# A four-layer graph network on one core: k's weight split on VectorE, x loaded later, output biases as two fp32r rows, and layer 2 that makes messages first

## The reference

```
x = LN(x + layer0(x))   # 8-head attention, bias from edge weights; two inner layer norms
x = LN(x + layer1(x))   # GCN: relu(segment_sum((x W)[src] * norm) + b)
x = LN(x + layer2(x))   # relational: h_all = x @ rel_W[r] + rel_b[r]; msg = h_all[src, type]
                        # agg = segment_sum(msg, dst) / max(deg, 1); LN(x + x self_W + self_b + agg);
                        # then gelu MLP 512-1024-512 and LN
x = LN(x + layer3(x))   # edge attention, 8 heads; MLP 512-256-512
```

## Time and profile before

| what | value |
|---|---|
| median of 3 runs | 628.55 us (623.87 to 629.28) |
| profiled execution, own time | 631.25 us |
| its span, first to last instruction | 629.5 us |
| mean granted TensorE clock | 0.959 |
| PE busy | 563.1 us (89%) |
| DVE busy | 384.2 us (61%) |
| ACT busy | 242.9 us (39%) |
| POOL busy | 238.4 us (38%) |

### The profile page before, as it was taken

One profiled execution on the slowest core, in us unless ns is written; L12 is line 12 of the kernel. 1 busy time (PEld: TensorE's weight loads), 2 busy tenths in 40 slices (PEclk: granted clock), 3 DMA queues, 4 the chain that ended last, 5 costly groups with the idle time before them and its releaser, 6 DMA issues.

```text
span 629.5 us, 7530 instructions
## 1 busy us (share of the span) xinstructions
PE 563.1 (89%) x2433; PEld 355.0 (56%) x2448; DVE 384.2 (61%) x939; ACT 242.9 (39%) x510; POOL 238.4 (38%) x210
## 2 busy tenths in 40 slices
PE   6998999993988999987999899996999998999691
PEld 2443444462843446666767688864877784445560
DVE  7986988993069868967646413134245416884736
ACT  3100700062247864573642221213433116885434
POOL 6565666668554004307213152333152664000000
PEclk8999999997999999997999899997999998999986
DMA  8720000022556000247222142244251844000001
GB/s 275 315 71 2 0 0 0 0 69 79 186 154 180 4 2 0 68 106 179 75 76 86 48 133 68 67 134 125 77 183 52 247 128 126 0 1 2 1 1 67
DMA packets 29383, 53.32 MB, mean 85 GB/s; under 512 B 4945, under 2 KB 6429, under 8 KB 28838
## 3 DMA queue, kind: packets, MB, share of 16 engines
q1 hardware_dynamic: 15436, 26.09, 14.0%
q0 software_dynamic: 11968, 19.96, 11.0%
q10 hardware_dynamic: 1946, 6.85, 3.3%
HBM read 50.73 MB, written 2.17 MB: 84 GB/s over the span
## 4 chain that ended last, share of the span: by engine, by line
PE 67%; DVE 17%; ACT 6%; issue 5%; POOL 2%; DMA 2%; ACTq 0%; DVEq 0%; POOLq 0%
PE bank L478 18%; PE bank L455 11%; PE bank L456 11%; PE bank L457 11%; PE bank L568 4%; PE bank L545 3%; PE bank L552 3%; DVE h L1040 2%; DVE sp L1193 2%; PE bank L447 2%; POOL edge_bias L364 1%; ACT waste L762 1%; ACT gap L762 1%; DVE h L1049 1%; DVE h L1048 1%
## 5 line engine op out<-in xcount | busy, mean ns | idle before, releaser
L341 POOL TENSOR_TENSOR wl<-wraw,wh 128x512 fp32r<-128x512 f32 (+1 forms) x82 | 106.9, 1324 | 98.7 <-DMA wh<-w 33.1
L478 PE MATMUL bank<-hot 128*128 128x512 bf16 x529 | 118.9, 383 | 5.6 <-DVE hot L1097 4.8
L478 PEld LDWEIGHTS bank<-hot 128*128 128x128 bf16 x544 | 53.4, 99 | 70.8 <-DVE hot L1097 6.2
L364 POOL DMA_INDIRECT edge_bias<-ewn,cell_at x68 | 76.5, 1125 | 44.3 <-DVE cell_at L1091 19.1
L455 PE MATMUL bank<-th,wl 128*128 128x512 f32 x104 | 43.4, 417 | 15.0 <-POOL wl L341 12.4
L455 PE MATMUL bank<-wh,tl 128*128 128x512 f32 x112 | 46.2, 412 | 3.0 <-DVE tl L1008 3.0
L457 PE MATMUL bank<-wh,th 128*128 128x512 f32 x112 | 44.4, 397 | 0.0
L456 PE MATMUL bank<-wl,th 128*128 128x512 f32 x112 | 44.4, 397 | 0.0
L456 PE MATMUL bank<-tl,wh 128*128 128x512 f32 x104 | 42.8, 411 | 0.0
L457 PE MATMUL bank<-th,wh 128*128 128x512 f32 x104 | 42.3, 407 | 0.0
L777 ACT ACTIVATE sp<-sp,peak 128x512 f32<-128x512 f32 x44 | 31.7, 720 | 25.7 <-DVE peak L1193 25.4
(11 more groups left out here) (194 smaller groups left out, 1083.2 us busy)
## 6 DMA issues: line engine op xcount, KB each, us to landing
wraw<-w SPq DMA_DIRECT2D x26, 256.0 KB, 2.9
wh<-w POOLq DMA_DIRECT2D x6, 1024.0 KB, 5.8
keyb<-edge_keys ACTq DMA_DIRECT2D x4, 1088.0 KB, 12.0
wh<-w_rel POOLq DMA_DIRECT2D x4, 1024.0 KB, 5.8
wraw<-w_rel SPq DMA_DIRECT2D x16, 256.0 KB, 2.7
wraw<-w_qkv SPq DMA_DIRECT2D x12, 256.0 KB, 6.4
wraw<-w_o SPq DMA_DIRECT2D x8, 256.0 KB, 3.0
wh<-w_o POOLq DMA_DIRECT2D x2, 1024.0 KB, 5.8
```

What stands on the lines that cost most here:

```text
L341: pool.tensor_tensor(wl[n % WSLOTS][:, k, 0:width], wraw[:, q % 3, 0:width], wh[n % WSLOTS][:, k, 0:width], ALU.subtract).then_inc(s["w_lo ...
L364: pool.indirect_dma_start(out=bias_dram, out_offset=bass.IndirectOffsetOnAxis(ap=cell_at[:, c:c + 1], axis=0), in_=ewn[:, c:c + 1], in_off ...
L478: mm = pe.matmul(ps(name)[:], hot[:, slot, 0, i * P:(i + 1) * P], hot[:, slot, 1 + kind, :], start=False, stop=last, skip_group_check=True)
```

## The change

1. **k's weight.** It leaves the list of raw quarters. Once POOL has taken the low part of x^T from `y`, SP loads all of w0_k into `y`; ACT rounds it early. DVE takes its low part after marking duplicates and ahead of unpacking. POOL's `low(1)` is gone.
2. **x's load** waits for `bias_loaded` too; ahead of it stands one more raw quarter.
3. **Output biases.** Each row is loaded twice, into two neighbouring partitions of `rows` (cleared by POOL). DVE makes `add2`: high part in the even, low part in the odd partition (`second` is -1 on odd partitions, so row = -high + raw). One fp32r matmul of 2 partitions takes the place of the fp32 matmul of 1. For layer 3's b3_2 the same is done on 2 partitions, and ACT issues its load later.
4. **Layer 2.** message(r, i) = x tile i times W_r (12 matmuls); DVE adds the relation's bias row to it in PSUM; ACT and DVE split it; gather(r, k) adds C_r's source tile k times the message tile to all four agg2 banks (12 matmuls). The degrees and L680 are gone, and so are DVE's two memsets and the split rows of x. The bias rows are broadcast to all partitions (4 x 256 KB), behind z1. `counth` of relation 0 is split after the layer norm, not ahead of z1's eviction; the mask's three parts are spread over rounds 1 to 3.

```diff
@@ SP
-            for q in range(3, 7):
+            raw(3)
+            eng.wait_ge(s["x_low"], K)
+            eng.dma_start(y[:], weights["w0_k"].rearrange("(k p) n -> p k n", p=P)).then_inc(s["ld_k"], 16)
+            for q in range(4, 7):
                 raw(q)
...
+            eng.wait_ge(s["rows_clear"], 1)
             for n, name in enumerate(("b0_o", "b0_1", "b2_self", "b2_2")):
-                eng.dma_start(par[32 * n:32 * n + 1, 4, :], rows_of[name]).then_inc(ld_par[4], 16)
+                eng.dma_start(rows[32 * n:32 * n + 2, :], rows_of[name].to_broadcast([2, D])).then_inc(s["ld_bias"], 16)
+            raw(7)
             eng.wait_ge(s["dups_done"], 1)
+            eng.wait_ge(s["bias_loaded"], 16)
             eng.dma_start(x[:], x0.rearrange("(i p) d -> p i d", p=P)).then_inc(s["ld_x"], 16)
...
-                    eng.wait_ge(s["deg_zero"], 1)
+                    wait_full(eng, ("z1", K - 1))
                     for r in range(4):
-                        eng.dma_start(rel_rows[32 * r:32 * r + 1, :], rel_b[r:r + 1, :]).then_inc(s["ld_rel"], 16)
+                        eng.dma_start(rel_add[:, r, :], rel_b[r:r + 1, :].to_broadcast([P, D])).then_inc(s["ld_rel"], 16)
@@ POOL
-            low(1)
@@ PE
-                row = slice(32 * n, 32 * n + 1)
-                pe.matmul(ps(name)[:], ones[row, :].bitcast(F32), par[row, 4, :], start=True, stop=False)
+                row = slice(32 * n, 32 * n + 2)
+                pe.matmul(ps(name)[:], ones[row, :], add2[row, :], start=True, stop=False)
...
+            def gather(r, k, tiles, last=False):
+
+                pe.wait_ge(s["msgl_ready"], T * r + k + 1)
+                pe.wait_ge(s["countl_ready"], T * r + k + 1)
+                for i in tiles:
...
+                    pe.matmul(ps(name)[:], countl[:, k, cut], msgh[:, r % 2, k, :], start=r == 0 and k == 0, stop=False)
+                    pe.matmul(ps(name)[:], counth[:, k, cut], msgl[:, r % 2, k, :], start=False, stop=False)
+                    mm = pe.matmul(ps(name)[:], counth[:, k, cut], msgh[:, r % 2, k, :], start=False, stop=last)
+                return mm
...
+            for i in range(T):
+                row_tile("self2", i, 6, 2, turned(1, i))
+                if i == 0:
+                    w_ready(7)
+                message(0, i)
+                if i < 2:
+                    turn(1, x, 3, i + 2)
+            for r in range(3):
+                w_ready(8 + r)
                 for k in range(T):
...
+                    message(r + 1, k)
+                    gather(r, k, range(T)).then_inc(s["msg_used"], 1)
+            for i in range(T):
+                for k in range(T):
+                    mm = gather(3, k, [i], k == T - 1)
+                finish(mm, ("agg2", i))
@@ ACT
+            def count_high(r, i):
+
                 if r:
...
+                    act.wait_ge(s["msg_used"], T * (r - 1) + i + 1)
+                act.copy(counth[:, i, :], counts[:, r // 2, r % 2, i, :]).then_inc(s["counth_ready"], 1)
@@ DVE
+            dve.wait_ge(s["ld_bias"], 64)
+            bias_rows(rows[:], slice(0, P), 0)
+            for f in range(K):
+                dve.wait_ge(s["k_high"], f + 1)
+                dve.tensor_tensor(wl[1][:, f, :], y[:, f, :], wh[1][:, f, :], ALU.subtract).then_inc(s["k_low"], 1)
...
-            count_low(0)
...
             for r in range(1, 4):
...
+                for i in range(T):
+                    message_add(r, i)
+                    if r == 1:
+                        mask_of(i)
+                    if r == 3:
+                        mask_and_log(i)
+                    message_low(r, i)
+                    count_low(r, i)
```

More of the change, by code:

```diff
@@ L97, in psum_plan @@
     tiles("turn1", 0)
-    n = 0
     for r in range(4):
-        for f in range(5):
-            use(("z2", r, f), 4 + n % 4)
-            n += 1
+        for i in range(4):
+            use(("msg", r, i), 4 + i)
     tiles("self2", 0)
@@ L131 @@
 W_LAST = {"w0_q": ("q0", 3), "w0_k": ("k0", 3), "w0_v": ("v0", 3), "w0_o": ("o0", 3), "w0_1": ("f0", 3), "w1": ("g1", 3),
-          "w2_self": ("self2", 3), "w2_rel3": ("agg2", 3), "w2_1a": ("hid2", 3), "w2_1b": ("hid2", 7), "w2_2a": ("f2", 3), "w2_2b": ("f2", 3),
+          "w2_self": ("self2", 3), **{f"w2_rel{r}": ("msg", r, 3) for r in range(4)}, "w2_1a": ("hid2", 3), "w2_1b": ("hid2", 7), "w2_2a": ("f2", 3), "w2_2b": ("f2", 3),
           "w3_q": ("q3", 3), "w3_k": ("k3", 3), "w3_v": ("v3", 3), "w3_o": ("o3", 3), "w3_1": ("hid3", 1), "w3_2": ("f3", 3)}
@@ L625, in _ @@
                     turn(1, x, 3, i - 2)
-            def source_ready(k):
-                if k >= 2:
-                    turn(1, x, 3, k)
-                pe.wait_ge(s["rowl_ready"], T + k + 1)
-                pe.wait_ge(s["countl_ready"], k + 1)
-            def degrees(r):
-                begin(("z2", r, 4))
-                for k in range(T):
-                    pe.matmul(ps(("z2", r, 4))[:], ones[:], countl[:, k, :], start=k == 0, stop=False)
-                    mm = pe.matmul(ps(("z2", r, 4))[:], ones[:], counth[:, k, :], start=False, stop=k == T - 1)
-                finish(mm, ("z2", r, 4))
@@ L809, in weight_high @@
                 act.copy(wh[n][:, k, :], wraw[:, q % 3, :]).then_inc(s["w_high"], 1)
-            for q in range(7):
+            for q in range(4):
+                weight_high(q)
+            act.wait_ge(s["ld_k"], 16)
+            for f in range(K):
+                act.copy(wh[1][:, f, :], y[:, f, :]).then_inc(s["k_high"], 1)
+            for q in range(4, 7):
                 weight_high(q)
@@ L1116, in _ @@
             dve.sem_inc(s["const_ready"], 1)
-            link(dve.memset(ones[:].bitcast(F32), 1.0))
+            link(dve.tensor_scalar(ones[:], iota[:, 0:P], 0.0, 1.0, ALU.mult, ALU.add))
             link(dve.memset(keyb[:, E:], -1.0))
@@ L1162, in _, with bias_rows @@
             dve.sem_inc(s["dups_done"], 1)
+            def bias_rows(raw, rows_, count):
+                dve.tensor_copy(add2[rows_, :], raw).then_inc(s["add2_ready"], 1)
+                dve.wait_ge(s["add2_ready"], count + 1)
+                dve.scalar_tensor_tensor(out=add2[rows_, :], in0=add2[rows_, :].bitcast(F32), scalar=second[rows_, :], in1=raw, op0=ALU.mult,
+                                         op1=ALU.add).then_inc(s["add2_ready"], 1)
+            dve.wait_ge(s["ld_ident"], 16)
+            link(dve.tensor_reduce(second[:], ident[:, 1::32], AX_X, ALU.add))
+            link(dve.tensor_scalar(second[:], second[:], -1.0, None, ALU.mult))
+            dve.wait_ge(s["ld_bias"], 64)
+            bias_rows(rows[:], slice(0, P), 0)
+            for f in range(K):
+                dve.wait_ge(s["k_high"], f + 1)
+                dve.tensor_tensor(wl[1][:, f, :], y[:, f, :], wh[1][:, f, :], ALU.subtract).then_inc(s["k_low"], 1)
             for b in range(8):
```

225 lines of the change are left out of this document (95 added, 130 removed).

## The result

| | before | after |
|---|---|---|
| median | 627.86 us (4 runs, 623.87 to 629.28) | 605.93 us (4 runs, 604.03 to 607.49) |
| profiled execution, own time | 631.25 us | 605.63 us |
| its span, first to last instruction | 629.5 us | 603.9 us |
| mean granted TensorE clock | 0.959 | 0.963 |

The ratio is 0.9667, with a 95% interval of 0.9618 to 0.9716. The forecast of 599.0 was 6.9 us too low; its range, 590 to 609, holds the time. The profiled executions differ by 25.6 us where the terms made 29.5. The medians differ by 21.9, because the profiled execution before lay 3.4 us above its median and the one after did not.

What follows compares the result with a forecast made beforehand. PE's matmuls were taken as the price in most stretches, its idle time as the rest. Terms 7.4 + 2.3 + 3.1 + 13.4 + 3.3 = 29.5 off the median 628.55 gave 599.0 us, range 590 to 609.

Steps and rivals of the forecast that it cites:

- k's split, 7.4: Ahead of attention: k no longer waits for POOL's scatters and subtractions, so scores start at 171.1, 7.4 us gained (4 to 10).
- the forecast's fear of it: Product v: its weight is ready between 155 and 161 while PE asks at 160, so PE might wait for it.
- o0 and the end of layer 1, 2.3 + 3.1: 2.3 us from o0's bias rows and DVE's memsets; 3.1 (1 to 4) from g1 following z1 directly.
- The 0.7 charged for collisions: End of layer 1: g1's tiles meet POOL's w2_self and rel0 subtractions on DVE's two-input adds, 0.7 us taken off.
- PE's work in layer 2, 18.4: Layer 2, PE alone: degrees, three rounds, mask round, idle time, L680 and self2's bias cost go, 18.4 us gained.
- its cover: Layer 2's added DVE and ACT work is hidden, each result used a round later, unless a step takes DVE over 5.44 us.
- The charge of 5 for DVE beside POOL: End of layer 2 and its norm: two POOL stretches block DVE's two-input operations, costing 5 us (0 to 9).
- The forecast's sign of a DVE operation of over 3 us in that norm: In the norm after layer 2, a DVE operation beside POOL would take over 3 us.
- w2_2b's lateness, charged at nothing: Behind layer 2: w2_2b's turn comes 2 us late, but not if the norm was late already; no cost charged.
- The biases, 3.3 each in self2 and f2: Four bias rows each in self2 and f2, 0.82 us saved per row, 3.3 us gained in each.
- late weights and the shared port take more: Rival: both POOL blocks at 9, attention's DVE operations hit, v's weight late; 16 to 22 us gained, 610; chance 0.18.

Runs made afterwards that it cites:

- counts_ahead: Changed kernel with relation 0's counts split ahead of z1's evictions again, not behind the layer norm; 609.65 us against 632.8 for the kernel before, ratio 0.9612.
- best2: Changed kernel with banks 0 to 3 unpacked first, POOL's cpl subtractions ahead of w2_self's transfer, and adds x + b behind layer 2's norm; 591.27 us, ratio 0.9409.
- dve_loaded: Changed kernel with three added DVE subtractions in each of 12 steps of layer 2; 608.19 us against 632.8 for the kernel before, ratio 0.9572.
- adds_later: Changed kernel with POOL's four adds x + b put behind the transfer of w2_1b instead of ahead of w2_1a's; 598.85 us, ratio 0.952.
- undo_k: Changed kernel with k's weight as raw quarters split by POOL again and x loaded early again (parts 1 and 2 undone); 610.88 us, ratio 0.9708.
- q_first: Changed kernel with DVE unpacking banks 0 to 3 ahead of the bias rows and k's low part; 602.93 us, ratio 0.9618.
- bias_fp32: Changed kernel with the bias matmuls plain fp32 on one partition again (part 3 undone); 611.43 us, ratio 0.9756.
- x_early: Changed kernel with x loaded as soon as duplicates are marked, the eighth raw quarter following it (part 2 undone); 602.99 us, ratio 0.9605.
- part4_only: Changed kernel with parts 1 to 3 undone, layer 2 as changed; 617.94 us against 627.79 for the kernel before, ratio 0.9867.

## Why the forecast came close, and what failed in it

- **k's split, 7.4.** Right. 8.3 in the trace, of which 1.3 was the sweep; undone, 7.3. The gap of 4.6 (4.47) and its 4.1 us of DVE work (3.9) were as priced, the slow matmuls nearly (2.2 for 1.8). That it came so close is partly luck, since kernels alike in this place gain between 4 and 8. v's weight was never late, so the forecast's fear of it, and part 2, weighed nothing.
- **o0 and the end of layer 1, 2.3 + 3.1.** Measured 5.8 from attention to g1's start, and 0.1 up to layer 2: 5.9 for 5.4. (The two pieces named for o0, 0.82 and 1.35, add up to 2.2 and not 2.3.) counts_ahead puts 3.7 on the one piece. The 0.7 charged for collisions was not seen as such; the small mistakes went both ways. Here, too, there is luck in the match: from o0 to layer 2 the change takes 64.1 us, and four kernels that are alike in this stage 63.2 to 66.8, against 70.4 before.
- **PE's work in layer 2, 18.4.** With POOL kept out (best2), layer 2 and its norm take 129.0 - 110.6 = 18.4 us less. As a sum this term was exact, and dve_loaded shows that its cover was real. Inside it self2's bias rows gave 2.5 and not 3.3, so the rest gave 0.8 more than priced.
- **The charge of 5 for DVE beside POOL: mis-sized.** It cost 112.9 - 110.6 = 2.3. I had leaned to the row of 5.62, but that row belongs to one place, where it stands in every run; nowhere in layer 2's norm did DVE wait for four. The forecast's sign of a DVE operation of over 3 us in that norm did not come, though the norm was longer, as it had said. By the Trainium skill (SBUF — State Buffer, Who interferes with whom), an exclusion of one whole instruction, the charge would have been 2 to 3: in layer 2 the traces agree with it (1.66, 1.34 and 1.63 us beside POOL, where 0.75 is usual), at 243.11 they do not (5.62). The page speaks of the whole instruction; that it is never longer was the forecast's reading.
- **w2_2b's lateness, charged at nothing: the step that failed.** The forecast saw that its turn comes 2 us late and excused it by the norm being late as well. The norm was late, by 2.3 us, but the chain of weights that starts from the mask's last part was longer than priced. The forecast's own links (a transfer landing after 6.0 us, four subtractions in 5.2) make 44.8 us for four weights; in the profile the four took 48.6, the last one 13.3, with subtractions slowed beside DVE and waits for raw quarters. It ended 7 us into f2: 3.56 us of waiting and matmuls at the lower clock behind it, 5.6 together by adds_later. The size varies: of the nine kernels with this order on POOL seven waited 3.35 to 4.54 us, but undo_k and q_first 1.50 and 1.11, with f2 to the scores in 63.4 and 63.1 us and not 67 to 69.
- **The biases, 3.3 each in self2 and f2.** The mechanism was right, the price 0.62 a row and not 0.82, since the matmul behind the row follows after 0.43 and not 0.23: 2.5 in self2 and 2.1 in f2 by bias_fp32.
- **The sum.** Measured against forecast: 14.2 for 12.8 up to layer 2, 16.1 for 13.4 in it, -3.6 for +3.3 in f2, and 1.1 lost in small pieces elsewhere, 25.6 for 29.5. Set on the median, 628.55 - 25.6 is 603; the remaining 3 us to 605.9 are the profiled execution of before, which overstated the kernel. Errors of 6.9 in f2 and of -2.7 in layer 2 partly cancelled, and that is luck; with f2's wait as short as in q_first the time would have been some 4 us nearer to the forecast.

The rival "late weights and the shared port take more" had the right cause in its name only, late weights: none of what it priced (both blocks at 9, attention's operations hit, v's weight late) came. The time lay between its 610 and the forecast.

## What to carry to other kernels

When a change moves a signal to the end of a stage, follow everything queued behind the wait for it, to its last link: here four unhurried adds held five weights up, and moving them was worth more (5.6 us) than the engine block (2.3) I had priced so carefully. A block seen once in a trace is the property of a place until it is seen at another; try to move one of the two sides away, as one transfer moved did here, before pricing it elsewhere. And when a gap is closed ahead of a stage that is bound by other engines, look whether the gain still stands at the stage after it: unpacking first gained 4.3 us at the scores and none that shows at the end.

## What the runs showed of the hardware

- Four POOL subtractions beside two-input DVE operations: in one place, layer 0's norm, DVE's L1021 (L1040 before) started 0.04 to 0.07 us ahead of them and waited for all four (5.60 to 5.62 us, in all ten kernels that have this place). In layer 2's norm and with POOL's row moved they took turns, DVE 0.93 to 1.66 us each and POOL 5.9 to 6.1 for its four. Starts 0.06 us apart did not make the block in two other places (x_early at 431.02, before at 341.88).
- A bias matmul of 2 partitions in fp32r holds the next matmul off for 0.40 to 0.43 us, though its neighbours follow at 0.23; in fp32 on 1 partition 1.05.
- With a gap of 4.5 us closed, the granted clock was 0.75 and 0.79 in two stretches of the following attention (0.72 in both in best2), where the kernel with the gap had 1.00 in both. It is no rule: bias_fp32 has the gap and one such stretch.
- Within f2 the matmuls of the change follow at 0.233 us at a granted clock of 1.00, before the change at 0.228. bias_fp32 and part4_only have 0.233, too, so neither the form of the bias rows nor k's weight makes it; why was not found out.
